# The adapter layer's mask moves from VectorE and two full-array products to bf16 products on four column tiles of TensorE, and the order inside a step changes

## The chip, the cores and the metric

One core of a Trainium2 chip runs one program. The metric is the device time of one execution, in microseconds, median over several executions.

## The reference

A decoder of three layers over 16 sequences of 128 positions and width 256. The change touches the second, the adapter attention (called B in the kernel):

```python
q, k, v = heads(x @ Wq), heads(x @ Wk), heads(x @ Wv)        # 32 heads of 8
scores = rope(q) @ rope(k).T / sqrt(8) + attention_mask      # mask: 128x128 per sequence
scores = maximum(scores, finfo.min)
out    = softmax(scores) @ v
a_k, a_v = heads(ctx @ Wk), heads(ctx @ Wv)                  # the context, no mask
out   += tanh(gate) * softmax(q @ a_k.T / sqrt(8)) @ a_v
x = layernorm(x + out @ Wo)
```

The first layer (A) is a causal attention of 16 heads, the third (C and D) an attention with heads of 128 and a small mixture of experts. The masks of B are given as data, with values of 0 and -1e9.

## The kernel before

Layers A and B are one software pipeline written out by hand in **steps** `s`. In each step every engine runs its own function (`pe_ab`, `dve_ab`, `act_ab`, `pool_ab`, `sp_ab`), in a fixed order of calls, and waits on semaphores only. Work is cut into **units** of four heads, 512 columns: units 0 to 63 are A, units 64 to 319 are B. A sequence has 16 units in B: eight with the mask (`kd` 0) and eight against the context (`kd` 1, no mask). In B two units go together, one pair every second step, so that the pairs n, n+1 start in step s = n. "A step" of B is called a pair step below: two values of `s`.

- **Pass 1** (L554) computes query x key scores in bank n % 2. VectorE takes the maximum of each row (`maxima`, L737). In a masked unit the mask is first written into the bank by two products of an identity and the two fp32r parts of the mask (`MKh`, `MKl`, L547).
- **The shift**: when all maxima of a sequence are there, `shift_parts` on GpSimd splits them in three bf16 parts, TensorE turns them (L565), ScalarE copies them to `nmT` (L971), and SyncE moves them as rows into the stack `STK` beside the queries (four transfers a sequence, L1154).
- **Pass 2** (L589) computes key x query scores less that shift, 28 steps after pass 1, in bank 2 + n % 2. For a masked unit VectorE then adds the turned mask `MT` from the bank into `PT` (`mask2`, L746), and ScalarE takes the exponential in place (L978); for the others ScalarE does so from the bank (L985).
- **pv** (L611) multiplies by the values two steps after pass 2 with 32 columns of weights for each head, so that four heads stand side by side in four column tiles of the array.

The step on TensorE is pass 1, pass 2, pv, and then background work: transposes (L489, L621, L631), projections and the output product (L472 to L474). Units n % 4 share `PT`, units n % 2 a bank, so that pass 2 of a unit waits for the work of the unit two before, and its exponential for the pv of the unit four before.

The masks of two sequences (number `c`) are loaded and clamped, split into `MKh` on ScalarE (L963) and `MKl` on GpSimd (L1090), and turned once on TensorE (L512) and copied (L935). All transfers are issued by SyncE, in program order. Every one has the line L1154, and only their tiles tell them apart: `Bdrq`, `Bdrk`, `Bdra` are the DRAM copies from which queries, keys and context keys come back as rows of the stack.

Of the kernel before, what the change touches and what calls it, by code (L numbers as in the profile page):

```python
# [6 lines left out]
F32 = mybir.dt.float32  # L7
F32R = mybir.dt.float32r
# [35 lines left out]
def program(nc, I, out):  # L44
# [42 lines left out]
    identr = sb("B_identr", [128, 128], F32R, st_ab)  # L87
    MKh = [sb(f"B_MKh{i}", [128, 2, 128], F32R, st_ab) for i in range(2)]
    MKl = [sb(f"B_MKl{i}", [128, 2, 128], F32R, st_ab) for i in range(2)]
# [10 lines left out]
    gt = sb("B_gt", [128, 36], F32, st_ab)  # L100
    tabsA = VPOOL[:, 224:248, :].rearrange("p (t a) b -> p t (a b)", t=6)
# [12 lines left out]
    MT = [gap[0][:, 512 + 256 * i:768 + 256 * i].rearrange("p (b k) -> p b k", b=2) for i in range(2)]  # L114
# [12 lines left out]
    tabs_ready = ("ld_A", 32), ("ld_B", 16)  # L127
# [6 lines left out]
    LAST_FIRST = 292  # L134
# [42 lines left out]
    def v_masked(n):  # L177

        u = n - NA
        return 8 * (u // 16) + u % 16 + 1  # L180
# [21 lines left out]
    def shift_sem(g):  # L202
        return (f"shift_A{g % 4}", 16 * (g // 4 + 1)) if g < 16 else (f"shift_B{g % 2}", 64 * ((g - 16) // 2 + 1))
# [22 lines left out]
    STEPS = NN + 28 + 2 + 12  # L226
# [17 lines left out]
    clamps = {s - (6 if c < 10 else 7): c for s, (c, _) in masked.items()}  # L244
    vals = places((3, 5), (0, 14, 8, 16), (19, 22, 20, 25), (6, 22, 26, 30))
# [65 lines left out]
    def small_products(s):  # L311
# [6 lines left out]
        if s in masked:  # L318
            yield "mt", masked[s][0]
# [122 lines left out]
    def shift_parts(e, q, g, name):  # L442
# [6 lines left out]
        heads = lambda a: a[:, :, :].rearrange("p k (g h) -> p k g h", h=16)  # L449
# [8 lines left out]
    def pe_ab(e, steps):  # L458
# [49 lines left out]
        def masks(c):  # L508
            q.wait_ge("clamp", c - 7)
            o = turn(("mt", c), "mt_act", c - 7)  # L510
            for b in range(2):
                m = e.transpose(o[:, b * 128:b * 128 + 128], MK[c % 2][:, b, :], ident[:, :])  # L512
            m.then_inc(sem("mt_pe"), 1)

        def values(c, n, b):
# [8 lines left out]
            m.then_inc(sem("v_pe"), 1)  # L524

        def pass1(ns):
            for n in ns:
# [10 lines left out]
                if not L:  # L538
                    q.wait_ge("identb", 1)
# [19 lines left out]
        def shift(g):  # L559
            L = g // 16  # L560
            q.wait_ge(*(("sh_pool", 4 * g - 60) if L else ("sh_dve", 4 * g + 4)))
            q.wait_ge("identb", 1)
            gv = turn(("sh", g), "sh_act", g + 1)[:, :].bitcast(BF16)
            for kd in range(NK[L]):
                m = e.transpose(gv[0:3 * NH[L], kd * 128:kd * 128 + 128], nmb[L][:, kd, :, :, :].rearrange("p g a b -> p (g a b)"), identb[:, :])  # L565
            m.then_inc(sem("sh_pe"), 1)

        def pass2(ns):
            for n in ns:
                L, b, kd, t, i, hs = unit(n)  # L570
                if LAST_FIRST <= n < LAST_FIRST + 2:
                    q.wait_ge("m_dve", NN)
                elif n >= 2:
                    m_ = n - (2 if n < LAST_FIRST else 4)
                    if m_ >= NA and unit(m_)[2] == 0:
                        q.wait_ge("mt_dve", v_masked(m_))
                    else:
                        q.wait_ge("e_act", m_ + 1)
                if not L:
                    q.wait_ge("identb", 1)  # L580
# [3 lines left out]
            for j in range(4):  # L584
                for n in ns:
                    L, b, kd, t, i, hs = unit(n)
                    i3 = b % len(QS[L])
                    rows, h = (slice(64 * t, 64 * t + 54), hs[j] % 16) if L else (slice(0, 99), hs[j])
                    m = e.matmul(bank2(n)[:, j * 128:j * 128 + 128], (AS if kd else KS[L])[i3][rows, h, :], QS[L][i3][rows, h, :],  # L589
                                 start=bool(L), stop=bool(L) or j == 3, skip_group_check=not L)  # L590
# [62 lines left out]
        for s in steps:  # L653
            if pass1_units(s):
                pass1(pass1_units(s))
            if pass2_units(s):
                pass2(pass2_units(s))
            for n in pv_units(s):
                pv(n)
# [10 lines left out]
            if s in masked:  # L670
                masks(masked[s][0])
# [29 lines left out]
    def layernorm_power(e, q, ln, name, base=0, slots=8):  # L701
        k = base + ln % slots
        q.wait_ge("mhalf", 1)
# [8 lines left out]
    def dve_ab(e, steps):  # L712
# [1687 lines left out]
```

## Time and profile before

| what | value |
|---|---|
| executions shown | 1193.44, 1193.47, 1193.86 us (median 1193.47) |
| span of the profiled execution | 1193.7 us |
| VectorE busy, share of the span | 83% |
| TensorE busy, share of the span | 95% |
| B's pairs, first maxima to last | 177.2 to 526.5 us |

The profiled execution's span, from its first instruction to its last, lies within the times of the executions: nothing outside the span has to be added. TensorE's busy time is a union of matmuls whose ends are modelled and overlap, so it tells little of how full the engine is. What tells more is the time from one group's start to the next group's start in the timeline.

### The profile page before, as it was taken

To read this page: it belongs to the slowest core of one execution; us is meant where nothing else is said; L and a number is where in the kernel's file an instruction comes from. 1 tells how busy PE (TensorE), PEld (TensorE's weight loads), DVE (VectorE), ACT (ScalarE), POOL (GpSimd) and SP (SyncE) were. 2 spreads that over 40 slices of the span, in tenths; PEclk is the share of its full clock that TensorE was granted. 3 is DMA by queue.
4 is the path that set the end of the run, shared out by engine and by line. 5 is a ranking of instruction groups with operands and counts; after the bars stand their busy time and mean duration, and the time that the engine had idled before them with its cause. 6 is when DMAs were issued, how large, how long until landed. Compare 5 with 4: busy or idle time off the path is not lost.

```text
span 1193.7 us, 29551 instructions
## 1 busy us (share of the span) xinstructions
PE 1128.8 (95%) x11172; PEld 934.4 (78%) x11172; DVE 993.6 (83%) x2284; ACT 660.4 (55%) x1687; POOL 656.9 (55%) x706
## 2 busy tenths in 40 slices
PE   5899999899999999879999999999999999999997
PEld 5667666666776766546899899998999899997887
DVE  6768887888889898978888888888888888877977
ACT  5466554566766667565555444444444444558663
POOL 4467655545455455254778544544554454847665
PEclk9899999999999999999999999999999999999999
DMA  6875443334333433212222000000000100101111
GB/s 161 205 186 135 122 125 87 87 95 116 88 106 101 106 97 97 76 58 76 68 63 63 1 1 2 1 1 2 1 1 1 37 1 1 37 18 37 36 36 36
DMA packets 98670, 76.68 MB, mean 64 GB/s; under 512 B 73547, under 2 KB 86987, under 8 KB 98529
## 3 DMA queue, kind: packets, MB, share of 16 engines
q1 hardware_dynamic: 98529, 74.80, 23.1%
q8 instruction: 89, 1.46, 0.5%
q14 instruction: 52, 0.43, 0.1%
HBM read 53.86 MB, written 19.92 MB: 62 GB/s over the span
## 4 chain that ended last, share of the span: by engine, by line
PE 58%; DVE 23%; issue 7%; ACT 5%; POOL 3%; SPq 2%; DMA 2%; DVEq 0%; POOLq 0%; ACTq 0%
PE bank L1518 5%; DVE B_nr L737 4%; PE bank L1519 4%; PE bank L1520 4%; PE bank L1574 4%; PE bank L1547 4%; PE bank L611 4%; DVE PT L746 3%; PE bank L472 2%; PE bank L554 2%; SPq L1154 2%; PE bank L1534 2%; PE bank L1589 2%; PE bank L1587 2%; PE bank L1588 2%
## 5 line engine op out<-in xcount | busy, mean ns | idle before, releaser
L1822 POOL TENSOR_TENSOR C_QK<-C_t1b,C_t2b 128x512 f32<-128x512 f32 x128 | 168.9, 1320 | 226.6 <-DVE C_t2b L1661 226.0
L1658 DVE SCALAR_TENSOR_TENSOR C_t1b<-bank,C_bcol,C_tabs 64x512 f32<-64x512 f32 x256 | 192.0, 750 | 37.3 <-PE bank L1520 33.2
L737 DVE TENSOR_REDUCE B_nr<-bank 128x4 f32<-128x512 f32 x256 | 164.4, 684 | 22.6 <-PE bank L554 21.0
L1518 PE MATMUL bank<-C_XTh,C_Wh 128*128 128x512 f32 x256 | 111.9, 437 | 4.4 <-DVE C_t2b L1661 1.9
L985 ACT ACTIVATE PT<-bank 128x512 f32<-128x512 f32 x160 | 92.2, 598 | 39.8 <-PE bank L589 39.3
L1754 ACT ACTIVATE C_P<-bank,C_nm 128x128 f32<-128x128 f32 x256 | 90.7, 367 | 34.0 <-DVE C_nm L1671 32.4
L978 ACT ACTIVATE PT<-PT 128x512 f32<-128x512 f32 x96 | 59.3, 630 | 88.7 <-DVE PT L746 88.7
L1773 ACT ACTIVATE C_V<-bank 128x512 f32<-128x512 f32 x64 | 38.1, 597 | 124.1 <-PE bank L1536 122.5
L611 PE MATMUL bank<-PT,vpool 128*32 128x128 f32 x2048 | 97.4, 285 | 4.3 <-ACT PT L978 3.1
L1519 PE MATMUL bank<-C_XTl,C_Wh 128*128 128x512 f32 x256 | 101.2, 395 | 0.0
L1520 PE MATMUL bank<-C_XTh,C_Wl 128*128 128x512 f32 x256 | 100.8, 394 | 0.0
L1661 DVE SCALAR_TENSOR_TENSOR C_t2b<-bank,C_bcol,C_tabs 128x512 f32<-128x512 f32 x128 | 96.1, 751 | 1.8
L554 PEld LDWEIGHTS bank<-stk 48*128 48x128 bf16 (+1 forms) x1280 | 50.9, 96 | 52.3 <-issue 27.5
L554 PE MATMUL bank<-stk 48*128 48x128 bf16 (+1 forms) x1280 | 77.7, 221 | 9.6 <-DVE B_nr L737 8.9
L589 PE MATMUL bank<-stk 54*128 54x128 bf16 (+1 forms) x1280 | 76.5, 219 | 10.0 <-DVE PT L746 3.8
L1762 ACT ACTIVATE C_OTh<-bank,C_bcol 128x512 fp32r<-128x512 f32 x64 | 44.1, 690 | 73.6 <-PE bank L1574 73.0
L1682 DVE SCALAR_TENSOR_TENSOR C_OTl<-bank,C_bcol,C_OTh 128x512 fp32r<-128x512 f32 x64 | 47.9, 748 | 38.9 <-ACT C_OTh L1762 38.8
L705 POOL TENSOR_TENSOR rstd<-ve,mhalf 128x1 f32<-128x1 f32 x48 | 28.1, 584 | 91.1 <-DVE ve L699 91.1
L589 PEld LDWEIGHTS bank<-stk 54*128 54x128 bf16 (+1 forms) x1280 | 53.5, 95 | 27.8 <-DVE PT L746 6.8
L1534 PE MATMUL bank<-C_Wh,C_XTh 128*128 128x256 f32 x256 | 72.5, 283 | 1.6 <-DVE C_t2b L1661 1.3
L1587 PE MATMUL bank<-C_Wh,C_OTh 128*128 128x256 f32 x256 | 72.0, 281 | 0.4 <-DVE C_OTl L1682 0.4
L1535 PE MATMUL bank<-C_Wl,C_XTh 128*128 128x256 f32 x256 | 71.9, 281 | 0.0
(267 smaller groups left out, 3683.5 us busy)
## 6 DMA issues: line engine op xcount, KB each, us to landing
Adrq<-PB SPq DMA_DIRECT2D x16, 192.0 KB, 3.2
Adrk<-PB SPq DMA_DIRECT2D x16, 192.0 KB, 3.4
stk<-Adrq SPq DMA_DIRECT2D x16, 192.0 KB
stk<-Adrk SPq DMA_DIRECT2D x16, 192.0 KB
Bdrq<-PB SPq DMA_DIRECT2D x16, 192.0 KB, 2.7
stk<-Bdrq SPq DMA_DIRECT2D x32, 96.0 KB
Bdrk<-PB SPq DMA_DIRECT2D x16, 192.0 KB, 2.7
stk<-Bdrk SPq DMA_DIRECT2D x32, 96.0 KB
```

The lines of the kernel that those rows point to most:

```text
L554: m = e.matmul(bank[n % 2][:, j * 128:j * 128 + 128], QS[L][i3][rows, h, :], (AS if kd else KS[L])[i3][rows, h, :], start=bool(kd), stop=b ...
L589: m = e.matmul(bank2(n)[:, j * 128:j * 128 + 128], (AS if kd else KS[L])[i3][rows, h, :], QS[L][i3][rows, h, :], start=bool(L), stop=bool( ...
L611: m = e.matmul(o[32 * j:32 * j + 32, c3 * 128:c3 * 128 + 128], vp[:, h, :], pt_of(n)[:, j * 128:j * 128 + 128], start=first or not L, stop ...
L737: e.tensor_reduce(dst, bank[n % 2][:, :].rearrange("p (a b) -> p a b", a=4), AX.X, ALU.max, negate=True).then_inc(sem("m_dve"), 1)
L1518: e.matmul(o[:, :], CWh[hp][:, cs], XCh[0][:, t, :], start=t == 0, stop=False)
L1519: e.matmul(o[:, :], CWh[hp][:, cs], XCl[0][:, t, :], start=False, stop=False)
L1520: m = e.matmul(o[:, :], CWl[hp][:, cs], XCh[0][:, t, :], start=False, stop=t == 1)
L1534: e.matmul(ob, XCh[0][:, t, xs], CWh[hp][:, cs], start=t == 0, stop=False)
L1587: e.matmul(o, OCh[:, bs], CWh[hp][:, cs], start=r == 0 and b % 2 == 0, stop=False, skip_group_check=True)
L1658: e.scalar_tensor_tensor(out=v4(t1b[kq][lo:lo + 64, :]), in0=v4(o[hi:hi + 64, :]), scalar=bc[hi:hi + 64, :], in1=tabsC[hi:hi + 64, 2 * kq ...
L1661: e.scalar_tensor_tensor(out=v4(t2b[kq][:, :]), in0=v4(o[:, :]), scalar=bc, in1=tabsC[:, 2 * kq, :].unsqueeze(1).to_broadcast([128, 4, 128 ...
L1822: e.tensor_tensor(QK[v % 3][:, kq, :], t1b[kq][:, :], t2b[kq][:, :], ALU.add).then_inc(sem("rc_pool"), 1)
```

## The change

- Pass 1 and pass 2 of a masked unit both begin with four products that write the mask into the bank (`mask_by_rows`): weights are `pick`, 96 rows by 32 columns of 0 and 1, the moving operand is 512 columns (128, read four times) of the mask in three bf16 parts stacked on 96 rows, and the output goes to 32 partitions, one column tile of the array, each. `mask2` on VectorE is gone, and every exponential of B is taken from the bank.
- For that the masks are split in three bf16 parts (ScalarE and GpSimd, two operations each), written to DRAM and read back in the order (row in group, part) on 96 partitions, once as they are (`MP`) and once turned (`MTP`, six bf16 transposes instead of two fp32 ones): four more transfers for every two sequences.
- From step 64 on the order on TensorE is pv, masks of pass 2, masks of pass 1, pass 2, pass 1, and then the background. Pass 2 comes 26 steps after pass 1 instead of 28, pv 30 steps after it as before: four steps instead of two lie between pass 2 and pv.
- The parts of the shift are laid out by half first, so that a sequence's shift needs two transfers of six rows instead of four of three.
- `identr` and its copy are gone, a few waits have other names, and the scratch space for dynamic transfers is set to 8192.

```diff
-    LAST_FIRST = 292
+    LAST_FIRST = 294
...
-        return [s - 12] if 12 <= s < NA + 12 else pair(s - 28)
+        return [s - 12] if 12 <= s < NA + 12 else pair(s - 26)
...
-        return pass2_units(s - 2)
+        return [s - 14] if 14 <= s < NA + 14 else pair(s - 30)
...
+    mask_parts = [{s + k: c for s, c in clamps.items()} for k in (1, 2, 3, 4)]
+    masks_out = {s + 5: c for s, c in clamps.items()}
+    mask_turns = {s + (1 if c < 10 else 3): c for s, (c, _) in masked.items()}
+    masks_t_out = {bg0(c) + 28: c for c in range(8, 16)}
...
+        def mask_by_rows(o, parts, b):
+
+            for g in range(4):
+                e.matmul(o[32 * g:32 * g + 32, :].rearrange("p (a b) -> p a b", a=4), pick[:, :],
+                         parts[0:96, g, b, :].unsqueeze(1).to_broadcast([96, 4, 128]), start=True, stop=False, skip_group_check=True)
+
+        def mask1(n):
+            b = unit(n)[1]
+            c = 8 + b // 2
+            if n >= 2:
+                q.wait_ge("m_dve", n - 1)
+            q.wait_ge("ld_B", 48)
+            q.wait_ge(*parts_ready("mp_in", c))
+            mask_by_rows(bank[n % 2], MP[c % 2], b % 2)
...
-                elif not kd:
-                    q.wait_ge("identr", 1)
-                    q.wait_ge("mkl_pool", b // 2 + 1)
-                    for k, part in enumerate((MKh, MKl)):
-                        e.matmul(scores, identr[:, :], part[(b // 2) % 2][:, b % 2, :].unsqueeze(1).to_broadcast([128, 4, 128]),
-                                 start=k == 0, stop=False, skip_group_check=True)
...
         for s in steps:
+            if s >= NA:
+                for n in pv_units(s):
+                    pv(n)
+                for n in pass2_units(s):
+                    if is_masked(n):
+                        mask2(n)
+                for n in pass1_units(s):
+                    if is_masked(n):
+                        mask1(n)
+                if pass2_units(s):
+                    pass2(pass2_units(s))
             if pass1_units(s):
                 pass1(pass1_units(s))
...
-        def mask2(n):
-            L, b, kd, t, i, hs = unit(n)
-            v4 = lambda a: a.rearrange("p (a b) -> p a b", a=4)
-            q.wait_ge("mt_act", b // 2 + 1)
-            q.wait_ge("t_pe", n + 1)
-            q.wait_ge("pv_pe", pt_free(n))
-            e.tensor_tensor(v4(pt_of(n)[:, :]), v4(bank2(n)[:, :]),
-                            MT[(b // 2) % 2][:, b % 2, :].unsqueeze(1).to_broadcast([128, 4, 128]), ALU.add).then_inc(sem("mt_dve"), 1)
...
-            for n in pass2_units(s):
-                if n >= NA and unit(n)[2] == 0:
-                    mask2(n)
...
             for hg in range(1 + L):
-                for kd in range(NK[L]):
-                    row = 64 * hg + 48 + 3 * kd if L else 96
-                    load(QS[L][b % (5 if L else 10)][row:row + 3, :, :], nmT[L][b % 2][48 * hg:48 * hg + 48, kd, :],
-                         shift_sem(g)[0])
+                row = 64 * hg + 48 if L else 96
+                load(QS[L][b % (5 if L else 10)][row:row + 3 * NK[L], :, :], nmT[L][b % 2][:, hg, :], shift_sem(g)[0])
```

On TensorE, two masked pair steps in the middle of B stand in a row like this before the change (the end of one step's pass 2 and pv, the next step's masks and passes; `stk` is the stack, `vpool` the values):

```order
L589 MATMUL bank<-stk 128x128 x8
L611 MATMUL bank<-PT,vpool 32x128 x4
L611 MATMUL bank<-stk,vpool 32x128 x4
L547 MATMUL bank<-B_MKh,B_identr 128x512
L547 MATMUL bank<-B_MKl,B_identr 128x512
L547 MATMUL bank<-B_MKh,B_identr 128x512
L547 MATMUL bank<-B_MKl,B_identr 128x512
L554 MATMUL bank<-stk 128x128 x8
L589 MATMUL bank<-stk 128x128 x8
L611 MATMUL bank<-PT,vpool 32x128 x8
```

With the change pv is L640, the masks L541, pass 2 L618 and pass 1 L583. The rows are the step in which both passes are masked, and the one behind it:

```order
L640 MATMUL bank<-PT,vpool 32x128 x4
L640 MATMUL bank<-stk,vpool 32x128 x4
L541 MATMUL bank<-B_MTP,B_pick 32x512 x8
L541 MATMUL bank<-B_MP,B_pick 32x512 x8
L618 MATMUL bank<-stk 128x128 x8
L583 MATMUL bank<-stk 128x128 x8
L640 MATMUL bank<-PT,vpool 32x128 x8
L541 MATMUL bank<-B_MP,B_pick 32x512 x8
L618 MATMUL bank<-stk 128x128 x8
L583 MATMUL bank<-stk 128x128 x8
```

Pass 1 has moved from the head of the step to the end of its passes; between its maxima and the next pass 1 there now stand pv, the masks and pass 2.

On SyncE, where the second sequence of a pair of sequences gets its shift, the queue is this before (`B_nmT` is the shift):

```order
L1154 DMA stk<-Bdrq 8x2048
L1154 DMA Bdrk<-PB 128x6x128 x2
L1154 DMA stk<-B_nmT 3x16x128 x4
L1154 DMA stk<-Bdrk 24x1x2048
L1154 DMA stk<-Bdrk 16x1x2048
L1154 DMA stk<-Bdrk 8x2048
```

and with the change this:

```order
L1188 DMA stk<-Bdrq 8x2048
L1188 DMA B_MP<-Bmask 96x4x256
L1188 DMA Bdrk<-PB 128x6x128 x2
L1188 DMA stk<-B_nmT 6x16x128 x2
L1188 DMA stk<-Bdrk 24x1x2048
L1188 DMA stk<-Bdrk 16x1x2048
```

The masks' return from DRAM stands ahead of the keys' parts and of the shift, and the shift is two transfers.

## Rows read from the trace of the kernel before

**Rows 1.** Busy time by stretch: from, to, length, PE, PEld, DVE, ACT, POOL, clock, DMA share.
```profile
226.00:482.30 256.30, 246.83 (x3844) 176.50 (x3839) 225.71 (x435) 173.96 (x446) 130.56 (x169) 1.00 0.37 99
482.30:526.50 44.20, 37.91 (x621) 24.56 (x621) 40.86 (x88) 24.91 (x50) 13.41 (x20) 0.96 0.27 79
```

**Rows 2.** Groups of one period, 346.63 to 389.75 us.
```profile
L737 DVE TENSOR_REDUCE B_nr<-bank 128x4 f32<-128x512 f32 x32 | 20.5, 684 | 1.8 <-PE bank L554 1.6
L746 DVE TENSOR_TENSOR PT<-bank,stk 128x512 f32<-128x512 f32 x12 | 7.8, 679 | 0.0
L554 PE MATMUL bank<-stk 48*128 48x128 bf16 x128 | 6.4, 218 | 0.7 <-DVE B_nr L737 0.5
```

**Rows 3.** TensorE's timeline, starts of pass 1 over one period, some of seventeen.
```profile
346.63 0.40 PE L554 MATMUL bank<-stk 48*128 48x128 bf16 x8
...
354.63 0.40 PE L554 MATMUL bank<-stk 48*128 48x128 bf16 x8
357.60 0.40 PE L554 MATMUL bank<-stk 48*128 48x128 bf16 x8
...
365.60 0.40 PE L554 MATMUL bank<-stk 48*128 48x128 bf16 x8
367.91 0.40 PE L554 MATMUL bank<-stk 48*128 48x128 bf16 x8
...
375.72 0.40 PE L554 MATMUL bank<-stk 48*128 48x128 bf16 x8
378.99 0.40 PE L554 MATMUL bank<-stk 48*128 48x128 bf16 x8
...
387.16 0.40 PE L554 MATMUL bank<-stk 48*128 48x128 bf16 x8
389.77 0.40 PE L554 MATMUL bank<-stk 48*128 48x128 bf16 x8
```

**Rows 4.** TensorE's timeline, from pv over the mask products to the next pass 1.
```profile
379.94 0.43 PE L611 MATMUL bank<-PT,vpool 128*32 128x128 f32 x8
380.18 0.42 PE L611 MATMUL bank<-stk,vpool 128*32 128x128 f32 x8
380.54 0.50 PE L547 MATMUL bank<-B_MKh,B_identr 128*128 128x512 f32 x1
...
381.67 0.40 PE L554 MATMUL bank<-stk 48*128 48x128 bf16 x8
```

**Rows 5.** TensorE's timeline, background behind pv, in order of time.
```profile
374.08 0.39 PE L472 MATMUL bank<-B_Wh,OTh 128*128 128x256 f32 x1
374.31 0.28 PE L473 MATMUL bank<-B_Wl,OTh 128*128 128x256 f32 x1
...
375.50 0.28 PE L474 MATMUL bank<-XTh,B_Wl 128*128 128x256 f32 x1
```

**Rows 6.** TensorE's timeline, a light masked step: pass 1 and the next second mask.
```profile
400.70 0.40 PE L554 MATMUL bank<-stk 48*128 48x128 bf16 x8
...
402.54 0.50 PE L547 MATMUL bank<-B_MKh,B_identr 128*128 128x512 f32 x1
```

**Rows 7.** VectorE's timeline, the maxima of that pass 1.
```profile
401.19 1.29 DVE L737 TENSOR_REDUCE B_nr<-bank 128x4 f32<-128x512 f32 x2 [0.40 <-PE bank L554]
```

**Rows 8.** SyncE's queue, one sequence's shift.
```profile
408.94 3.06 SPq L1154 DMA_DIRECT2D stk<-B_nmT  x4
```

**Rows 9.** TensorE's timeline, a step near the end of B.
```profile
502.31 0.40 PE L554 MATMUL bank<-stk 48*128 48x128 bf16 x8
...
505.11 0.48 PE L547 MATMUL bank<-B_MKh,B_identr 128*128 128x512 f32 x1 [0.80 <-DVE B_nr L737]
...
506.81 0.50 PE L554 MATMUL bank<-stk 48*128 48x128 bf16 x6
```

**Rows 10.** VectorE's timeline where B ends and C has begun.
```profile
545.77 1.89 DVE L746 TENSOR_TENSOR PT<-bank,stk 128x512 f32<-128x512 f32 x3 [0.31 <-PE bank L589]
...
548.29 1.52 DVE L1658 SCALAR_TENSOR_TENSOR C_t1b<-bank,C_bcol,C_tabs 64x512 f32<-64x512 f32 x2
```

More of the change, by code:

```diff
@@ L100, in program @@
     gt = sb("B_gt", [128, 36], F32, st_ab)
+    pick = sb("B_pick", [96, 32], BF16, st_ab)
+    MQ = sb("B_MQ", [128, 3, 2, 128], BF16, st_ab)
+    MR = sb("B_MR", [128, 2, 128], F32, st_ab)
+    MTP = [sb(f"B_MTP{i}", [96, 4, 2, 128], BF16, st_ab) for i in range(2)]
+    MTQ = sb("B_MTQ", [128, 3, 2, 128], BF16, st_ab)
     tabsA = VPOOL[:, 224:248, :].rearrange("p (t a) b -> p t (a b)", t=6)
@@ L126, in program @@
                for i in range(2)] for k in RW[L]} for L in range(2)]
-    tabs_ready = ("ld_A", 32), ("ld_B", 16)
+    mask_dram = [nc.dram_tensor(f"Bmask{i}", [128, 768], BF16, kind="Internal").ap() for i in range(2)]
+    by_rows = lambda a: a.rearrange("(g r) (j x) -> (r j) g x", g=4, j=3)
+    tabs_ready = ("ld_A", 32), ("ld_B", 48)
     ot = I["c_one"]
     NA, NN = 64, 320
-    LAST_FIRST = 292
+    LAST_FIRST = 294
     def unit(n):
@@ L175, in k_val, with is_masked, parts_ready @@
         return 2 * c + b if c < 8 else 16 + 4 * (c - 8) + ((0, 2, 1, 3) if c < 10 else (0, 1, 2, 3))[2 * n + b]
-    def v_masked(n):
-        u = n - NA
-        return 8 * (u // 16) + u % 16 + 1
+    def is_masked(n):
+        return n >= NA and unit(n)[2] == 0
+    def parts_ready(name, c):
+        return name, 32 * (c - 7)
     def stack_left(i, k):
@@ L202, in shift_sem @@
     def shift_sem(g):
-        return (f"shift_A{g % 4}", 16 * (g // 4 + 1)) if g < 16 else (f"shift_B{g % 2}", 64 * ((g - 16) // 2 + 1))
+        return (f"shift_A{g % 4}", 16 * (g // 4 + 1)) if g < 16 else (f"shift_B{g % 2}", 32 * ((g - 16) // 2 + 1))
     def on_v(og, k):
@@ L317, in small_products @@
             yield ("pj",) + projs[s]
-        if s in masked:
-            yield "mt", masked[s][0]
+        if s in mask_turns:
+            yield "mp", mask_turns[s]
         if s in vals:
@@ L506, in project, with mask_parts_turned @@
                 m.then_inc(sem("pj_pe"), 1)
[L508 to L512, printed above, removed]
+        def mask_parts_turned(c):
+            q.wait_ge("mq_pool", 2 * (c - 7))
+            o = turn(("mp", c), "mt_act", c - 7)[:, :].bitcast(BF16)
+            for part in range(3):
+                for b in range(2):
+                    k = 2 * part + b
+                    m = e.transpose(o[:, k * 128:k * 128 + 128], MQ[:, part, b, :], identb[:, :])
             m.then_inc(sem("mt_pe"), 1)
@@ L524, in values, with mask2 @@
             m.then_inc(sem("v_pe"), 1)
+        def mask_by_rows(o, parts, b):
[10 more added lines that the diff above has]
+            mask_by_rows(bank[n % 2], MP[c % 2], b % 2)
+        def mask2(n):
+            b = unit(n)[1]
+            c = 8 + b // 2
+            bank2_free(n)
+            q.wait_ge("ld_B", 48)
+            q.wait_ge(*parts_ready("mtp_in", c))
+            mask_by_rows(bank2(n), MTP[c % 2], b % 2)
         def pass1(ns):
@@ L570, in pass2 @@
                 L, b, kd, t, i, hs = unit(n)
[L571 to L578, printed above, removed]
+                bank2_free(n)
                 if not L:
-                    q.wait_ge("identb", 1)
+                    q.wait_ge("consts", 1)
                     e.matmul(bank2(n)[:, :].rearrange("p (a b) -> p a b", a=4), identb[:, :],
@@ L588, in pass2 @@
                     rows, h = (slice(64 * t, 64 * t + 54), hs[j] % 16) if L else (slice(0, 99), hs[j])
+                    alone = bool(L) and not is_masked(n)
                     m = e.matmul(bank2(n)[:, j * 128:j * 128 + 128], (AS if kd else KS[L])[i3][rows, h, :], QS[L][i3][rows, h, :],
-                                 start=bool(L), stop=bool(L) or j == 3, skip_group_check=not L)
+                                 start=alone, stop=alone or j == 3, skip_group_check=not alone)
                     if j == 3:
@@ L669, in pe_ab @@
                     project(*projs[s], 1)
-            if s in masked:
-                masks(masked[s][0])
+            if s in mask_turns:
+                mask_parts_turned(mask_turns[s])
             if s in vals:
@@ L1035, in act_ab @@
                 x_high(*xts[s - 1])
-            if s - 1 in masked:
-                masks(masked[s - 1][0])
-                mask_high(masked[s - 1][0])
+            if s - 1 in mask_turns:
+                mask_parts_turned(mask_turns[s - 1])
+            for part in range(2):
+                if s in mask_parts[2 * part]:
+                    mask_part(mask_parts[2 * part][s], part)
             if s - 1 in vals:
@@ L1118, in pool_ab @@
                 add_adapter(tos[s - 2][0])
-            if s - 2 in masked:
-                mask_low(masked[s - 2][0])
+            for part in range(2):
+                if s in mask_parts[2 * part + 1]:
+                    mask_rest(mask_parts[2 * part + 1][s], part)
             for part in range(2):
@@ L1467, in norm_pool @@
     def norm_pool(e, q, c):
[L1468 removed]
+        q.wait_ge("consts", 2)
         q.wait_ge("cn_bn", 9 * c + 9)
```

128 lines of the change are left out of this document (80 added, 48 removed).

## The prediction

> **What bounds the kernel now.** The change touches layer B alone, so I read first the busy times by stretch. In the steady part VectorE is busy 225.7 of 256.3 us and TensorE, by its modelled ends, nearly always; towards the end VectorE is busy 40.9 of 44.2 us and TensorE's clock dips to 0.96 [rows 1]. Two engines near their limit: which of them sets the pace must be read step by step. The groups of one period (two sequences, 16 pair steps) say what VectorE would lose: 12 of the 16 mask additions take 7.8 us, so 16 take 10.4, of 43.1 [rows 2, 3]. A reader who stops here expects a quarter of VectorE's time to turn into a large gain. The timeline of TensorE says otherwise. I take each slot from one start to the next. Eight pv products take 0.24 us, the last eight before another kind of product 0.36; four mask products of 512 columns take 1.13, which is 4 x 0.235 and twice 0.1 [rows 4]. The background behaves alike: its first product takes 0.23 and its last 0.22, the ten between 0.12 each [rows 5]. So each switch of the array's division (rows for the passes, columns for pv, whole for the rest) costs 0.1 to 0.2, and a step holds about 0.4 of it, beside 0.46 for the passes and 0.48 for pv.
>
> With these slots a step with full background is explained without any wait: 0.94 + 0.4 + 12 products at 0.12 is 2.78, and the three steps from 367.91 to 375.72 (4, 12 and 12 small products or transposes) come to 7.6 against 7.81 [rows 3, 5]. TensorE is the bound there. In the three light masked steps of each half it is not: they take 8.00 and 8.17 us, 2.7 each, for some 2.2 of work [rows 3]. There a loop holds: pass 1 starts at 400.70, its maxima at 401.19, two of them last 1.29, and at 402.54 the second unit's mask begins; 1.84 us from pass 1 to there, whatever else is done [rows 6, 7].
>
> **The change, part by part.**
>
> *Mask products.* Out: 32 whole-array products of a period, 32 x 0.235 = 7.5 us. In: 16 masked units, each with a group of four column products in both passes, 32 groups. No row has bf16 products of 512 columns on column tiles. The bounds: if the four run side by side, a group takes as long as one product of that length, 0.235; if not at all, four times that, 0.94. The nearest row is pv, four column tiles at a time: eight products in 0.24, while a full-width product of 256 columns takes 0.12 [rows 4, 5], so the tiles do run side by side there. I take 0.235: TensorE's mask work is unchanged in sum (7.5), and moves: pass 1 gives back 0.47 a pair, pass 2 gets 0.47 a pair.
>
> *The order.* A switch is saved only where no whole-array background stands in the step (three of 16 steps: 0.2 each, 0.6). The six mask transposes instead of two add about 0.35 - 0.19.
>
> *Now the steps of one period.* (a) Six light steps, 16.17 us before. The loop is now: 1.84 to the second mask, its 0.235, a switch 0.1, pass 2 0.23, then pass 1: 2.40. Before it was 1.84 + 0.47 + 0.1 and the switch's rest, 2.5. Six steps at 2.4, one with the mask transposes at 2.5, make 14.5: -1.6. (b) Six steps that get pass 2's masks (346.63 to 354.63 and 367.91 to 375.72, 15.81 us) are full with projections: + 6 x 0.47 = 2.8, less the 0.7 that pass 1 waited for maxima in the period [rows 2, 3]: +2.1. (c) The remaining four, 43.14 - 16.17 - 15.81 = 11.2 us, keep a mask pair (the step with both has 0.94 as before) and lose the jitter of VectorE: by the slots 2 x 3.0 + 2 x 2.34 = 10.7: -0.5. Sum: 0.0 us a period. **VectorE's 10.4 us buy nothing in the steady part**, because the work lands in steps that TensorE already fills, and the light ones are held by pass 1 and its maxima.
>
> *Start.* While the first sequences pass through pass 1 and pass 2 has not begun, their masks cost half, 8 pairs x 0.47 = 3.8, part of which the loop keeps: -2.
>
> *End.* Without projections VectorE is the bound [rows 1]. In the step at 502.31 pass 1 comes again only after 4.50 us: the mask addition and a residual stand before the maxima, and TensorE waits 0.80 [rows 9]. TensorE's work there is 3.0. Two such steps give 1.0 and 1.5, the six light ones about 0.4 each, the last of the passes 1: together -6. Behind B's last maxima, four mask additions from 545.77 hold VectorE until layer C's rotation starts at 548.29 [rows 10]; with the exponentials freed from VectorE as well, -3. The masks' 1.9 us of TensorE in that stretch lie in its gaps. End: -9.
>
> *Transfers.* One shift costs SyncE 3.06 us for four transfers [rows 8], now about 1.5; four mask transfers are added per two sequences at about 0.5 to 0.7 each. The queue is no longer than before; the return of the masks waits for their arrival in DRAM, a short wait. They are read ten or more steps later. Costed at nothing; if that cover is gone, a late shift holds pass 2, see below. ScalarE's and GpSimd's extra parts (about 1 us a period each) are covered by their idle time.
>
> *Sum:* 0 - 2 - 9 = -11 from the profiled span of 1193.7 us, which is the median of the runs to 0.3: **1182.5 us**. Its own range is 1176 to 1189: 0.9 us a period either way in the steady part (5.9 periods [rows 1]).
>
> **A rule weighed against the rows.** In the rows, pv's column tiles overlap fully (eight in 0.24 [rows 4]). The Trainium skill, in "TensorE: Matmul & The Clock Gate", Part 3 on packing small matmuls, says that a weight load overlaps running matmuls only when its row group differs, and gives 3.07x for four row tiles of 512 columns. By the rule's figure the mask groups would take 4 / 3.07 of 0.235, an estimate of 0.31, and the sum would be 1202; by the row it is 1182.5. All mask groups share the same rows, as pv's do, so the rule speaks against pv's rows too.
>
> **The rivals.**
>
> *Column tiles overlap less for 512 columns (slower than before).* For it: no row has this product, and its operand is four times as long. Against: pv. Place: the 256 groups of the kernel. From +0.043 us a group (0.278 instead of 0.235) it eats the 11 us; at a third more, 0.31, it adds 256 x 0.078 = 20: 1202. With no overlap, 256 x 0.7 = 180: 1362. Chance 0.07.
>
> *VectorE was the bound all through.* If the waits seen in light steps and the six full steps are all VectorE's, removing 10.4 us lets each period fall to TensorE's work, about 40.3: -2.8 x 5.9 = -16 more, 1166. For it: 225.7 of 256.3 us busy. Against: the slots of full steps. Chance 0.10.
>
> *A late shift.* Pass 2 asks for the shift two steps (2.7 us) earlier, and its two transfers stand behind the masks' return and the keys' parts. Half the transfers give back 1.5. If it comes 1 us late for each of 16 sequences: +16, 1198; from 0.7 us it decides the sign. For it: the lag is shorter; against: the exponentials and splits ahead of it no longer wait for VectorE. Chance 0.05.
>
> *The end gains little.* ScalarE's own work for layer C and the exponentials hold the end, not VectorE: -3 to -5 in all, 1190. Chance 0.10.
>
> The forecast itself 0.65, something unnamed 0.03.
>
> **Numbers.** 1182.5; range 1172 to 1193, which leaves out most of the first rival, the second and the third, 2 in 10. Within 0.2% (2.4 us) is what a measurement of this kernel can hardly tell from no change. Faster by more: 0.65 + 0.10 + 0.06 = 0.81; within: 0.08 (part of the fourth, a steady part that loses 1.5 us a period); slower: 0.11.
>
> **What would show it.** Period of 16 pair steps near 43.1 us again; light masked steps near 2.4 us; mask groups of eight column products in 0.47 us; the three steps behind pass 2's masks longer by up to 0.47; VectorE's idle time up by some 10 us a period with TensorE still without gaps in the full steps; the step near the end at 3 us instead of 4.5. Wrong, if the period falls to 41 or less (then the loop or the switches are cheaper than I read them), if the eight mask products take clearly over 0.5, or if pass 2 waits for a transfer.

## The result and the profile after

The changed kernel takes 1206.8 us (median of six executions, 1199.1 to 1207.9) beside 1193.7 for the kernel before (1193.4 to 1198.4). The ratio over all executions is 1.0092, its 95% interval 1.0067 to 1.0116, which is 8 to 14 us. By the medians it is slower by 13 us where I forecast 11 us faster. The profiled execution took 1207.9 us, its span is 1206.1.

Busy time by stretch answers to [rows 1]; the columns are the same. The first two rows are B's steady part and its end, between the same steps as there; the others are single stretches of 43 us within the steady part.

```profile
231.50:501.60 270.10, 249.60 (x4448) 174.31 (x4443) 173.05 (x342) 178.09 (x453) 132.10 (x174) 0.96 0.40 112
501.60:542.00 40.40, 36.91 (x744) 22.96 (x742) 30.57 (x70) 26.14 (x54) 16.24 (x26) 1.00 0.25 79
...
351.00:394.00 43.00, 40.75 (x702) 29.04 (x703) 26.63 (x54) 26.72 (x72) 21.46 (x29) 0.92 0.39 110
394.00:437.00 43.00, 40.09 (x709) 28.40 (x706) 28.22 (x57) 28.30 (x74) 20.23 (x26) 0.96 0.41 113
437.00:480.00 43.00, 39.61 (x730) 28.08 (x728) 29.53 (x59) 29.95 (x77) 21.91 (x30) 1.00 0.42 115
```

VectorE has lost some 50 us (225.7 to 173.1), as meant. But the stretch takes 270.1 us instead of 256.3, and TensorE's granted clock, 1.00 in it before, is now 0.96, and 0.92 in one of the shorter stretches. Something is new, and it is found by laying the starts of pass 1 side by side, step by step. Over two sequences (32 steps, 16 pair steps), fifteen pair steps take much what they take in the kernel without the stall (experiment 6), but for some slow ones right behind the sixteenth. That one, step 20 of 32, takes 4.25 to 5.58 us from step 148 on. This is TensorE's timeline there, with 5.58:

```profile
396.01 0.39 PE L583 MATMUL bank<-stk 48*128 48x128 bf16 x8
396.33 0.31 PE L594 MATMUL bank<-identb,B_nmb 128*96 128x128 bf16 x2
396.48 0.50 PE L650 MATMUL bank<-ident,OTf 128*128 128x128 f32 x3
398.59 0.80 PE L524 MATMUL bank<-identb,B_MQ 128*128 128x128 bf16 x6 [1.62 <-ACT B_nmT L1005]
399.32 1.08 PE L640 MATMUL bank<-PT,vpool 128*32 128x128 f32 x16
400.18 1.08 PE L541 MATMUL bank<-B_MP,B_pick 96*32 96x512 bf16 x8
401.19 0.61 PE L618 MATMUL bank<-stk 54*128 54x128 bf16 x8
401.59 0.59 PE L583 MATMUL bank<-stk 48*128 48x128 bf16 x8
```

The six mask transposes (L524) wait 1.62 us for a ScalarE copy (L1005) which isn't theirs: it is the copy of the shift. And from there the products are slow: sixteen pv products take 0.86 us from start to start, eight mask products 1.01. At the full clock they take 0.46 and 0.44 to 0.55. All are about twice as slow: that is the 1.2 GHz level. It doesn't come every time. The same wait ends at 305.98, 351.53, 398.59, 444.15 and 488.18 us; the clock fell at four of them, and at the fourth it didn't, where step 20 takes 4.25 us:

```profile
444.15 0.49 PE L524 MATMUL bank<-identb,B_MQ 128*128 128x128 bf16 x6 [1.61 <-ACT B_nmT L1005]
```

ScalarE's timeline shows what stands ahead of the copy:

```profile
396.21 0.60 ACT L1015 ACTIVATE PT<-bank 128x512 f32<-128x512 f32 x1 [0.73 <-PE bank L618]
396.70 0.59 ACT L1015 ACTIVATE stk<-bank 128x512 f32<-128x512 f32 x1
397.18 0.63 ACT L954 ACTIVATE PB<-ab 128x512 bf16<-128x512 f32 x1
397.70 0.49 ACT L1027 ACTIVATE OTf<-bank 128x384 f32<-128x384 f32 x1
398.07 0.38 ACT L1005 ACTIVATE B_nmT<-bank 96x256 bf16<-96x256 bf16 x1
```

Two exponentials, a split part, the copy of pv's bank, and then the shift's. The answer for the line L524 counts how often:

```profile
its engine sat idle before it (us, times) until:
  issue: 11.0, 7
  ACT B_nmT L1005: 8.1, 5
  DVE z L833: 1.6, 1
```

("issue" is here the loading of the weights, which waits beside its products; the wait for `z`, 1.56 us at 261.32, is for VectorE's residual, the bank's tenant there.) Why wait for someone else's copy? From step 86 on the small products of the background share a ring of two banks, handed out in the order in which they stand in the program (`bank[6 + len(home) % 2]`). A tenant may write when the one before it in its bank has been evacuated. Before, the mask's transposes stood at step 18, two steps ahead of the shift's. The change puts them at step 21. The ring then hands out: shift, turn of an output (both step 20), mask: the mask gets the shift's bank, one pair step behind it.

### The profile page after: what moved, and what is told of

It reads as the page before. It is cut to its first block, busy times and chain, and to the rows that moved or that the text cites. A ratio compares the mean times of both kernels' runs of the same rounds, so it can differ in the third digit from the quotient of the medians.

```text
span 1206.1 us, 30999 instructions
## 1 busy us (share of the span) xinstructions
PE 1131.8 (94%) x11972; PEld 930.8 (77%) x11972; DVE 919.9 (76%) x2155; ACT 661.5 (55%) x1695; POOL 661.0 (55%) x714
## 3 DMA queue, kind: packets, MB, share of 16 engines
q8 instruction: 95, 1.56, 0.5%
## 4 chain that ended last, share of the span: by engine, by line
PE 68%; DVE 17%; issue 5%; ACT 3%; POOL 3%; DMA 0%; SPq 0%; DVEq 0%; POOLq 0%; ACTq 0%
PE bank L640 5%; PE bank L1582 5%; PE bank L1583 4%; PE bank L1584 4%; PE bank L541 4%; PE bank L1638 4%; PE bank L1611 4%; PE bank L618 4%; DVE B_nr L778 4%; PE bank L482 3%; PE bank L583 3%; PE bank L483 2%; PE bank L484 2%; PE bank L1598 2%; PE bank L1653 2%
## 5 line engine op out<-in xcount | busy, mean ns | idle before, releaser
L1015 ACT ACTIVATE PT<-bank 128x512 f32<-128x512 f32 x256 | 145.8, 597 | 127.9 <-PE bank L618 127.3
L640 PE MATMUL bank<-PT,vpool 128*32 128x128 f32 x2048 | 98.5, 289 | 2.0 <-ACT OTf L1025 2.0
L618 PEld LDWEIGHTS bank<-stk 54*128 54x128 bf16 (+1 forms) x1280 | 49.4, 96 | 54.1 <-issue 43.7
L618 PE MATMUL bank<-stk 54*128 54x128 bf16 (+1 forms) x1280 | 77.2, 222 | 1.6 <-DMA stk<-A_nmT 1.4
L583 PE MATMUL bank<-stk 48*128 48x128 bf16 (+1 forms) x1280 | 77.3, 222 | 1.2 <-DVE B_nr L778 1.2
L450 POOL TENSOR_TENSOR PB<-y,PB 128x512 bf16<-128x512 f32 x36 | 42.5, 1182 | 56.1 <-ACT PB L957 55.8
L1600 PE MATMUL bank<-C_Wh,C_XTl 128*128 128x256 f32 x256 | 71.9, 281 | 0.0
```

Of the source, the lines that this page charges most:

```text
L583: m = e.matmul(bank[n % 2][:, j * 128:j * 128 + 128], QS[L][i3][rows, h, :], (AS if kd else KS[L])[i3][rows, h, :], start=bool(kd), stop=b ...
L640: m = e.matmul(o[32 * j:32 * j + 32, c3 * 128:c3 * 128 + 128], vp[:, h, :], pt_of(n)[:, j * 128:j * 128 + 128], start=first or not L, stop ...
L1015: e.activation(pt_of(n)[:, :], bank2(n)[:, :], ACT.Exp).then_inc(sem("e_act"), 1)
```

## The experiments

Each is measured beside the kernel before on the same chip: its median was 1194.4 us for experiments 1 to 4, 1193.6 for 5 to 8 and 1193.4 for 9 to 12. What is read from a trace holds for the profiled execution of a version.

**1. The mask's transposes earlier.** In the changed kernel:

```diff
-    mask_turns = {s + (1 if c < 10 else 3): c for s, (c, _) in masked.items()}
+    mask_turns = {s + (1 if c < 10 else 0): c for s, (c, _) in masked.items()}
```

> The changed kernel, with the six mask transposes of sequences 20 and up three steps earlier (step 18 of 32 instead of 21), where they no longer follow the shift's transposes in the bank that ScalarE's copy must free. Theory A (the waits on that bank, five times about 2.1 us, and the 1.2 GHz stretches that follow them make the loss): 10.5 us of waits and about 6 of clock go, 1188 us (1184 to 1192), no wait before the mask transposes above 0.5 us, light steps at 2.4. Rival B (the mask groups or the transfers themselves cost it): 1203 to 1208, only the place of the waits differs. Rival C (the clock falls in the light steps whatever stands there): the waits go, the clock stays low, 1195 to 1198.

Measured: 1191.0 us, ratio 0.9977 (0.9965 to 0.9988). The clock is 1.00 in every period of the steady part. The answer for L524 has only this left:

```profile
  issue: 0.2, 1
```

One number in one table turns a loss of 13 us into a gain of 3. Rivals B (the mask groups or the transfers cost it) and C (the clock falls in the light steps whatever stands there) fall.

**2. The same move alone, in the kernel before,** for its two mask transposes and their copy.

```diff
+    mask_turns = {s + (1 if c < 10 else 3): c for s, (c, _) in masked.items()}
...
-            if s in masked:
-                masks(masked[s][0])
+            if s in mask_turns:
+                masks(mask_turns[s])
...
```

> The kernel before, with one thing of the change: its two mask transposes, and ScalarE's copy of them, three steps later (step 21 of 32), behind the shift's transposes. Theory A: five waits of about 2.1 us and some clock, 1193.7 + 11 to 15, so 1205 to 1209. Rival B: the place of two transposes is worth nothing, 1193 to 1195.

Measured: 1211.7 us, ratio 1.0146 (1.0133 to 1.0160), +17, more than the 11 to 15 that I expected: the wait is 2.04 us here. The kernel before can be made slow by this move with none of the rest; step 20 takes 5.4 to 6.5 us instead of 2.8 (from step 148 on). Rival B falls a second time.

**3. The copy ahead in ScalarE's queue.** In the changed kernel:

```diff
-            if s - 1 in turned:
+            if s - 1 in turned and turned[s - 1] < 17:
                 shift(turned[s - 1])
...
             for n in pass2_units(s):
                 exps(n)
+            if s in turned and turned[s] >= 17:
+                shift(turned[s])
```

> The changed kernel, with ScalarE's copy of the shift taken out of its place behind a split part and the copy of pv's bank, and put straight behind the exponentials of the step; TensorE's order is untouched. Theory A: the bank comes free about 0.9 us earlier, five times, with a little of the clock: 1206.8 - 4.5 - 2, so 1200 (1197 to 1203), and the wait at the mask transposes shrinks from 2.1 to about 1.2 us but doesn't go. Rival B: 1206 to 1208. If the loss hangs on the clock alone and that needs a wait of over 1 us, it gains more, 1194.

Measured: 1194.3 us, ratio 0.9997 (0.9978 to 1.0016): 12.5 us less than the changed kernel, twice the gain that I expected. The wait:

```profile
386.47 0.49 PE L524 MATMUL bank<-identb,B_MQ 128*128 128x128 bf16 x6 [0.72 <-ACT B_nmT L1005]
386.90 0.64 PE L640 MATMUL bank<-PT,vpool 128*32 128x128 f32 x16
387.36 0.62 PE L541 MATMUL bank<-B_MP,B_pick 96*32 96x512 bf16 x8
```

The wait is 0.90 shorter, as said. But the sixteen pv products behind it take 0.46, not 0.86: the clock didn't fall. Step 20 takes 3.36 us where it took 5.58. This is the profiled execution, at 1189.6 us one of the fastest of twelve, with a mean clock of 0.992. The twelve go from 1188.0 to 1199.7 us at mean clocks of 0.993 to 0.983, so in the slower ones the clock did fall; where, no trace shows.

**4. Transfers.** The merged shift alone, in the kernel before, with its layout and transposes by head group.

```diff
...
-                for kd in range(NK[L]):
-                    row = 64 * hg + 48 + 3 * kd if L else 96
-                    load(QS[L][b % (5 if L else 10)][row:row + 3, :, :], nmT[L][b % 2][48 * hg:48 * hg + 48, kd, :],
-                         shift_sem(g)[0])
+                row = 64 * hg + 48 if L else 96
+                load(QS[L][b % (5 if L else 10)][row:row + 3 * NK[L], :, :], nmT[L][b % 2][:, hg, :], shift_sem(g)[0])
```

> The kernel before, with the merged shift alone (two transfers of 96 rows for each sequence in place of four of 48, transposes of 96 columns by head group). Theory A holds transfers hidden: 1193 to 1194. Rival D (the queue of SyncE is late in places, and the merge gives time back): 1188 to 1191. Rival E (larger transfers land later and pass 2 waits): over 1196.

Measured: 1195.4 us, ratio 1.0006 (0.9997 to 1.0016). Costed at nothing, worth nothing.

**5. The order and the lag alone**, in the kernel before.

```diff
-    LAST_FIRST = 292
+    LAST_FIRST = 294
...
-        return [s - 12] if 12 <= s < NA + 12 else pair(s - 28)
+        return [s - 12] if 12 <= s < NA + 12 else pair(s - 26)
...
+            if s >= NA:
+                for n in pv_units(s):
+                    pv(n)
+                if pass2_units(s):
+                    pass2(pass2_units(s))
             if pass1_units(s):
                 pass1(pass1_units(s))
...
```

> The kernel before, with the order and the lag of the change alone: pv first in a step, then pass 2, then pass 1, pass 2 one pair step earlier; the masks stay whole-array products and VectorE's additions. By the slots a switch of the array is saved in three of sixteen steps, 0.6 us a period, about 3 in all, unless pass 2 of a masked unit now waits for VectorE's addition: 1192 (1189 to 1197). Rival: the order alone makes the gain of the change without its stall, 1188 or less. Rival: the order alone costs, over 1198, because the maxima come behind the mask additions.

Measured: 1287.4 us, ratio 1.078 (1.0758 to 1.0803). A clear miss: +94 us; a rival that I had named at over 1198 is right in kind. TensorE, then VectorE:

```profile
457.82 0.40 PE L589 MATMUL bank<-stk 54*128 54x128 bf16 x8 [2.16 <-DVE stk L752]
```
```profile
455.19 1.29 DVE L743 TENSOR_REDUCE B_nr<-bank 128x4 f32<-128x512 f32 x2 [2.10 <-PE bank L554]
456.39 0.68 DVE L752 TENSOR_TENSOR PT<-bank,stk 128x512 f32<-128x512 f32 x1
456.99 0.68 DVE L752 TENSOR_TENSOR stk<-bank,stk 128x512 f32<-128x512 f32 x1
```

Pass 2 of a step is done before its pass 1, but VectorE takes the maxima first, and these wait 2.10 us for pass 1. The mask additions come behind them, and the next pass 2 waits 2.16 us for the additions. So the new order can't be had with VectorE's additions as VectorE's work is ordered now, and order and masks can't be priced one by one. Additions ahead of the maxima on VectorE were not tried.

**6. All mask transposes in their old steps,** those of the first two pairs of sequences too.

```diff
-    mask_turns = {s + (1 if c < 10 else 3): c for s, (c, _) in masked.items()}
+    mask_turns = {s: c for s, (c, _) in masked.items()}
```

> The changed kernel, with all mask transposes back in the steps they had before (the first two pairs of sequences as well). The bank ring then has the order of before. Theory A: beside the five waits it removes a sixth at step 88, where the values' products took the bank of a transposed input and waited 1.1 us for VectorE: the 1191.0 us of the run with only the later turns moved, less 2 to 3: 1188.5 (1187 to 1190). Rival: that wait only moves on, 1190.5 to 1191.5.

Measured: 1187.3 us, ratio 0.9939 (0.9925 to 0.9953). Step 88 takes 2.40 us instead of 5.97 in the changed kernel (4.09 in experiment 1). There the products of a projection had got the bank of a transposed input, and waited 1.08 us for VectorE's low part (experiment 1).

**7. GpSimd's part in the tail.** As 6, and:

```diff
-    HIGHS, LOWS = [308, 310, 342, 351], [322, 323, 351, 352]
+    HIGHS, LOWS = [308, 310, 342, 351], [317, 323, 351, 352]
```

> As the run with all mask transposes in their old steps, and with GpSimd's first low part of layer C's weights (2.35 us) at step 317 instead of 322, where GpSimd stood idle. Theory F: layer C's first projection waited 2.8 us for GpSimd, which made low parts for 4.7 + 2.5 us in a row, and this took the gain of the tail: 2 us faster than that run, 1186.5 (1185 to 1188). Rival: another engine holds the tail, no difference within 0.5 us.

Measured: 1183.2 us, ratio 0.9912 (0.9898 to 0.9925), 4.1 less than 6 where 2 were expected. In the changed kernel, TensorE and then GpSimd:

```profile
545.40 0.55 PE L650 MATMUL bank<-ident,OTf 128*128 128x128 f32 x3 [0.31 <-ACT OTf L1027]
548.72 0.71 PE L1582 MATMUL bank<-C_XTh,C_Wh 128*128 128x512 f32 x1 [2.77 <-issue]
```
```profile
541.50 4.68 POOL L1709 TENSOR_TENSOR C_Wl<-C_QK,C_Wh 128x1024 fp32r<-128x1024 f32 x2
546.14 2.48 POOL L1571 TENSOR_TENSOR C_XTl<-C_XF,C_XTh 128x512 fp32r<-128x512 f32 x2
```

"issue" names nobody, but GpSimd's low part ends at 548.62, and layer C's first projection starts at 548.72. Behind this wait the projection's six products take 0.42 to 0.43 each from start to start, the 1.2 GHz level again (0.51 for the first). With the low part early, in experiment 7, the wait is 0.48 and they take 0.23:

```profile
526.87 0.47 PE L1582 MATMUL bank<-C_XTh,C_Wh 128*128 128x512 f32 x1 [0.48 <-DVE rr L798]
527.18 0.39 PE L1583 MATMUL bank<-C_XTl,C_Wh 128*128 128x512 f32 x1
527.41 0.40 PE L1584 MATMUL bank<-C_XTh,C_Wl 128*128 128x512 f32 x1
```

**8. The old order with the new masks.** As 6, and (with the old lag):

```diff
...
-                for n in pv_units(s):
-                    pv(n)
...
+            for n in pass1_units(s):
+                if is_masked(n):
+                    mask1(n)
+            if pass1_units(s):
+                pass1(pass1_units(s))
+            for n in pass2_units(s):
+                if is_masked(n):
+                    mask2(n)
+            if pass2_units(s):
+                pass2(pass2_units(s))
+            for n in pv_units(s):
+                pv(n)
```

> As the run with all mask transposes in their old steps (masks by column tiles in both passes), but with the old order of a step (pass 1, pass 2, pv) and the old lag. By the slots the new order saves a switch in the light steps, 0.6 us a period, and keeps the second mask off the loop of pass 1 and the maxima: without it 3 to 5 us slower than that run, 1192 (1189 to 1196). Rival: the order is worth nothing, within 1 us of it.

Measured: 1185.6 us, ratio 0.9928 (0.9915 to 0.9940). I expected it 3 to 5 us slower than 6; it is 1.7 faster. A period takes 42.6 us (from 336.06 to 378.70) beside 43.2 in 6 between the same steps, with light steps at 2.21 in place of 2.33 to 2.40. My expectation has the wrong sign, and the rival, nothing within 1 us, is nearer. Why the old order suits the short groups better was not taken apart.

**9. Together:** as 8, with the line of 7.

> The three things that gained so far together: masks by column tiles, all mask transposes in their old steps, the old order and lag of a step, and GpSimd's first low part of layer C's weights at step 317. If they add up: 1185.6 for the old order, less the 4.1 us that the early low part gave in the new order, 1181.5 (1180 to 1184). Rival: in the old order the tail is held by the exponentials and not by GpSimd, then 1185.

Measured: 1182.4 us, ratio 0.9910 (0.9893 to 0.9927). The best version of the study beside 7, from which it can't be told.

**10. The old order, with the mask transposes at step 21:** as 8, with the `mask_turns` of the change.

> As the run in the old order (masks by column tiles, old order and lag), but with the mask transposes where the change put them, behind the shift's. Theory A says that the wait hangs on the bank and on ScalarE's queue, not on the order of the passes: five waits of about 2 us and the clock behind them, 1200 to 1206. Rival: with the old order the copy comes in time, under 1190.

Measured: 1196.3 us, ratio 1.0019 (1.0008 to 1.0031), 10.7 above 8, less than the 14 to 20 that I expected. The wait is there, but the clock is 1.00 from 233 to 540 us:

```profile
392.77 0.50 PE L524 MATMUL bank<-identb,B_MQ 128*128 128x128 bf16 x6 [1.25 <-ACT B_nmT L999]
```

**11. TensorE kept busy in the wait.** In the changed kernel, from the fourth pair of B's sequences on:

```diff
             q.wait_ge("mq_pool", 2 * (c - 7))
+            if c > 10:
+                for _ in range(16):
+                    e.matmul(bank[5][:, 384:512], identb[:, :], identb[:, :], start=False, stop=False, skip_group_check=True)
             o = turn(("mp", c), "mt_act", c - 7)[:, :].bitcast(BF16)
```

> The changed kernel, with sixteen idle products of 128 columns (identity by identity, into columns of a PSUM bank that nothing reads) ahead of the mask transposes of step 21, where TensorE waited 2.1 us anyhow. The wait for the bank stays. Theory C1 (part of the loss is the granted clock that falls to the 1.2 GHz level after each wait): the clock stays up, the interval of that step is 4.4 us instead of 5.3 to 5.6 and the next one 2.3 instead of 2.5 to 3.7: 7 us in all, 1200 (1197 to 1202). Rival C2 (the clock falls for another reason, in the light steps): no better than 1206.

Measured: 1198.9 us, ratio 1.0042 (1.0026 to 1.0058).

```profile
389.20 1.06 PE L522 MATMUL bank<-identb 128*128 128x128 bf16 x16
390.89 0.51 PE L527 MATMUL bank<-identb,B_MQ 128*128 128x128 bf16 x6 [0.63 <-ACT B_nmT L1008]
391.33 0.64 PE L643 MATMUL bank<-PT,vpool 128*32 128x128 f32 x16
391.79 0.62 PE L544 MATMUL bank<-B_MP,B_pick 96*32 96x512 bf16 x8
```

The bank comes no earlier, step 20 still takes 4.17 us, but behind it all is at the full clock and the next step takes 2.31. Useless products gain 8 us. Here too the executions differ, from 1194.3 to 1202.8 us at mean clocks of 0.991 to 0.984; the profiled one took 1195.6.

**12. VectorE loaded again.** As 6, and:

```diff
...
+            for n in pass2_units(s):
+                if is_masked(n):
+                    pads.append(n)
+                    q.wait_ge("pad_dve", len(pads))
+                    e.tensor_tensor(gap[0][:, 512:1024], gap[0][:, 512:1024], gap[0][:, 512:1024], ALU.add).then_inc(sem("pad_dve"), 1)
             if s - 1 in wos and s >= MASK_FIRST:
```

> As the run in the new order with all mask transposes in their old steps (1187.3 us), with VectorE loaded again: for each masked unit of pass 2 one addition of 512 columns on a scratch tile, where the mask addition stood, 128 in all, that nobody waits for. My prediction said that VectorE's time is worth nothing in the steady part and about 6 us in the end: 1187.3 + 4 to 6, so 1192 (1189 to 1194), the steady period within 0.5 us of 43. Rival (VectorE bounds the steady part): 10 us more a period, over 1230; a half of that, 1210.

Measured: 1228.8 us, ratio 1.0294 (1.0273 to 1.0315), +41.5 over 6: far above my forecast (1189 to 1194) and close to the total of the rival, though not by its 10 us a period. An addition took 0.83 us in the mean, more than the 0.68 of those removed [rows 2], so this loads VectorE with 106 us where 87 were taken off. VectorE and TensorE:

```profile
373.69 2.46 DVE L879 TENSOR_TENSOR stk<-stk 128x512 f32<-128x512 f32 x2
376.07 1.28 DVE L779 TENSOR_REDUCE B_nr<-bank 128x4 f32<-128x512 f32 x2
```
```profile
376.81 0.40 PE L541 MATMUL bank<-B_MP,B_pick 96*32 96x512 bf16 x4 [1.45 <-DVE B_nr L779]
377.41 0.40 PE L541 MATMUL bank<-B_MP,B_pick 96*32 96x512 bf16 x4 [0.20 <-DVE B_nr L779]
377.74 0.61 PE L618 MATMUL bank<-stk 54*128 54x128 bf16 x8
```

A period takes 46.1 and 46.8 us instead of 42.9 to 43.2. So 3 to 4 of the 13 us put on VectorE come through, because the maxima on which the next masks wait stand behind the additions. And again the clock falls behind the wait (0.96 in these periods). By stretch, 12 of the added us lie between steps 64 and 152, 16 from there to 286, 7 from there to 318, and 4 behind it.

## Why the prediction was wrong

**The step that failed** is "The six mask transposes instead of two add about 0.35 - 0.19". It costs the moved transposes as work, and says nothing on where they went. The move from step 18 to 21 is in the diff, and the bank ring is in the kernel: I had to ask whose bank they get, who empties it, and what stands ahead on that engine's queue. This was the very question that I had put to the shift's transfers (a rival that hardly occurred: in the changed kernel one weight load of pass 2 waits for it, 0.31 us at 533.26; in experiment 6, where the stall is gone, four do, by 0.30 to 0.64). What the step leaves out, by medians:

| part | us | from |
|---|---|---|
| waits for the bank, the one at step 88 included | 11.6 | experiments 11 and 6 |
| the clock behind the waits | 7.9 | changed kernel and experiment 11 |
| together | 19.5 | changed kernel and experiment 6 |

The medians split it only roughly, since the clock falls in some executions of experiment 11 too. The profiled executions split it by place:

| stretch, us | before | changed | experiment 11 | experiment 6 |
|---|---|---|---|---|
| start of the program to step 64 | 176.7 | 176.0 | 177.4 | 179.7 |
| steps 64 to 148 | 121.4 | 127.4 | 122.8 | 118.3 |
| steps 148 to 280, with the five waits | 177.9 | 191.4 | 182.6 | 177.1 |
| step 280 to the end | 717.7 | 711.3 | 711.0 | 711.3 |

Around the five waits the slower clock costs 8.8 us (changed less 11) and the waits themselves 5.4 (11 less 6). That is 1.1 a wait, less than the 4.17 - 2.33 = 1.84 by which step 20 is longer, because step 22 gives 0.7 back: it takes 3.05 us in experiment 6, where TensorE waits for VectorE's output, and 2.31 in 11.

```profile
387.73 0.38 PE L482 MATMUL bank<-B_Wh,XTh 128*128 128x256 f32 x1 [0.47 <-DVE ON L809]
```

In steps 64 to 148 the same two differences are 4.7 and 4.5. The 4.7 is nearly all chance: the changed kernel's clock was low from 217.7 to 231.4, from a wait of 1.18 us for maxima on, and its steps 88 and 92 took 5.97 and 5.59 us. Experiment 11 is the same kernel up to there, has that wait without the fall, and takes 4.09 and 3.19. The 4.5 are 1.7 at step 88 and 2.9 at step 116, where in experiment 11 the clock fell too (258.1). Without the step that failed the change is a gain of 6.4 us (1187.3), inside my range.

**The other steps,** read from experiment 6, where the stall is gone. These are its starts of pass 1 at the places of [rows 3]:

```profile
355.01 0.39 PE L583 MATMUL bank<-stk 48*128 48x128 bf16 x8
357.90 0.39 PE L583 MATMUL bank<-stk 48*128 48x128 bf16 x8
...
364.97 0.39 PE L583 MATMUL bank<-stk 48*128 48x128 bf16 x8
367.29 0.39 PE L583 MATMUL bank<-stk 48*128 48x128 bf16 x8
...
376.07 0.39 PE L583 MATMUL bank<-stk 48*128 48x128 bf16 x8
378.97 0.39 PE L583 MATMUL bank<-stk 48*128 48x128 bf16 x8
```

- *Mask groups.* Eight column products in a row, two groups, take 0.44 us where no switch follows (from 377.75 to 378.19 below): 0.22 a group, 0.235 predicted. The rival of tiles that overlap less is refuted: the four ran side by side, and the loads of the next four weights began at 377.76, under the products that had started at 377.75. The Trainium skill's 3.07x ("TensorE: Matmul & The Clock Gate", Part 3) is measured on four row tiles; carried over to these column tiles, as I had weighed it, it doesn't hold, nor does the rule on weight loads beside it.

```profile
377.75 0.62 PE L541 MATMUL bank<-B_MTP,B_pick 96*32 96x512 bf16 x8
378.19 0.61 PE L541 MATMUL bank<-B_MP,B_pick 96*32 96x512 bf16 x8
```

- *(a) Light steps.* 7.07 (from 357.90) and 7.42 (from 378.97, mask transposes included): 14.5, predicted 14.5.
- *(b) Full steps.* 8.75 (to 355.01) and 8.78 (from 367.29): 17.5 where 15.8 was before; +1.7, predicted +2.1. My check of these steps by slots was looser than I wrote: the three to 375.72 add up to 7.4 us, not 7.6, of 7.81, and 0.29 of the rest was a wait for maxima at 370.20.
- *(c) The rest.* 11.2 as before; 0.5 less was predicted. The period is 43.2 us in 6 (43.1 before), the others 42.9: the steady part gains 0.3 us a period at most.
- *VectorE's 10.4 us.* True as the sum of this change, in which the period didn't move. As a statement on the kernel it was too strong. With the additions left on VectorE the new order takes 55.3 us a period (experiment 5, from 376.22 to 431.56), so as VectorE's work is ordered now, the relief is what makes that order possible; and work put back where nobody waits for it still lengthens the period (experiment 12). In the old order (experiment 8) the new masks gain 0.5 to 0.8 us a period.
- *Order.* I gave it a saving of 0.6 us a period; with its lag it costs 0.5 (experiments 6 and 8).
- *Start.* In the profiled executions, from step 64 to 146 experiment 6 gains 2.7 us (-2 predicted), but the last part of layer A, where the first mask is now split in three, costs 1.3 to 1.9 (experiments 1 and 6), a term that I hadn't; that the split is the cause is not shown.
- *End.* 36.4 us from step 286 to 318 where 41.7 were before: -5.3, -6 predicted. Tail: -1.8 where I said -3, because GpSimd's chain took VectorE's place; with that chain opened (7) it is -5.4.
- *Transfers.* Nothing measurable, as costed (experiment 4 for the merged shift; the masks' transfers were not tested alone).
- *The base.* Every execution on record takes 1.8 us more than its span, so something does lie outside it: the profiled execution of before, with a span of 1193.7, took about 1195.5. Spans are compared with spans here. My 1182.5 is 1182.7 by its own terms.
- *The clock* was in no term. I took the slots of before, all at the full clock, as if they held whatever waits came.

So the mechanism of the slots held to some tenths of a us a step, and the sign was decided by one wait that I hadn't looked for, with the clock behind it. That the period came out as I said is partly luck: (b) was 0.4 us too high and (c) 0.5 too low, and the two cancel. What stays open: why the kernel with all turns home is 5 us above my sum is only partly shown (layer A, the order and the tail cover it in size, measured in single profiled executions).

## What to carry to other kernels

When a change moves an instruction, follow its bank or buffer before its cost: who held it last, on which engine that is evacuated, and what stands ahead in that engine's queue. Lay the starts of one repeated group side by side for both kernels, step by step: a stall that comes once in sixteen steps is lost in busy shares but stands out there. And price a wait on TensorE with what follows it: here five waits cost 5.4 us in all and the slower clock behind them another 8.8, and sixteen useless products in each wait took the 8.8 back (in the profiled executions; 7.9 us by the medians of the whole kernel).

## What the runs showed of the hardware

- Behind a wait of TensorE the clock can fall to the 1.2 GHz level, and the same wait does it in one place and not in the next. In the changed kernel it fell at four of five waits of 1.62 us, within the wait or up to 1.9 us behind its end in these cases and those that follow (over 3 us at that level each time), in experiment 2 at three of five of 2.04, in experiment 12 at three of four of 1.45. In the profiled executions of experiments 11 (0.63), 3 (0.72) and 10 (1.25) it fell at none of five. Other executions of 3 and 11 had lower mean clocks (down to 0.983 and 0.984), so these lengths are no safe bounds.
- Products of 512 columns on four column tiles of 32 run fully side by side: 0.22 us for a group of four, no more than one product over the whole array takes [rows 4].
- VectorE's additions of 512 columns with all operands in SBUF (experiment 12) took 0.69 us in the median and up to 1.74. Beside the pair that took 2.46, GpSimd's cast of 64 columns took 0.69 instead of 0.24. That the two engines held each other up is a guess; no run tests it.
